# Writing out TensorE's program for 25 tiles with fixed addresses, in place of a loop over a register

## The reference, cut to what matters

```python
h = relu(layernorm(x));  x = x + appnp(h)              # 10 steps: out = spmm(out)*0.9 + h*0.1
h = relu(layernorm(x));  x = x + gat(h, W, att, bias)  # softmax over each node's edges
h = relu(layernorm(x));  x = x + (h + attention(h))    # 4 heads, softmax over each node's edges
h = relu(layernorm(x));  x = x + mean(h[src] @ W + b)  # mean over each node's incoming edges
# spmm: msg = feat[col] * rsqrt(deg_row[row] * deg_col[col]); segment_sum(msg, row)
```

## Time and profile before

| what | value |
|---|---|
| median of 3 runs | 1796.67 us (1793.94 to 1797.15) |
| the profiled execution, its own time | 1796.92 us |
| its span, first to last instruction | 1795.0 us |
| busy share of the span: PE, PEld, DVE, ACT, POOL | 73%, 68%, 71%, 30%, 20% |
| mean granted clock of PE | 0.849 of full |
| counting stage (gathering and counting of all tiles) | about 85 to 373 us of the span |
| the ten steps (L1093) | from 393.6 us to about 922 us |

### The profile page before, as it was taken

One profiled execution on the slowest core, in us unless ns is written; L12 is line 12 of the kernel. 1 busy time (PEld: TensorE's weight loads), 2 busy tenths in 40 slices (PEclk: granted clock), 3 DMA queues, 4 the chain that ended last, 5 costly groups with the idle time before them and its releaser, 6 DMA issues. The chain is left out here.

```text
span 1795.0 us, 46599 instructions
## 1 busy us (share of the span) xinstructions
PE 1313.8 (73%) x18543; PEld 1223.3 (68%) x18544; DVE 1277.8 (71%) x2254; ACT 541.6 (30%) x1073; POOL 361.3 (20%) x202
## 2 busy tenths in 40 slices
PE   3678888849999999999955006777816777777458
PEld 3266777649999999999954005776715777676458
DVE  6876666655555455555565997999877999999832
ACT  0045555520000000000002862333314666666311
POOL 1400000000000000000000004888701555555300
PEclk6867666659999999999986557999858999999779
DMA  0012222258000000000002647555204333333093
GB/s 9 1 51 78 78 78 78 89 197 352 2 3 2 3 2 3 2 2 3 2 1 96 223 140 271 188 203 201 76 3 168 141 130 130 131 130 112 24 343 122
DMA packets 42985, 173.44 MB, mean 97 GB/s; under 512 B 14443, under 2 KB 16020, under 8 KB 42148
## 3 DMA queue, kind: packets, MB, share of 16 engines
q1 hardware_dynamic: 42452, 169.45, 26.0%
q0 software_dynamic: 336, 1.20, 0.2%
HBM read 127.19 MB, written 43.44 MB: 95 GB/s over the span
## 5 line engine op out<-in xcount | busy, mean ns | idle before, releaser
L1093 PE MATMUL psum<-work,count 128*128 128x192 f16 x6250 | 520.6, 247 | 29.6 <-issue 21.5
L1093 PEld LDWEIGHTS psum<-work,count 128*128 128x128 f16 x6250 | 519.0, 98 | 31.4 <-issue 21.7
L1588 PE MATMUL psum<-count 128*128 128x100 f16 (+1 forms) x1875 | 188.3, 208 | 87.8 <-DVE count L1685 61.4
L1038 DVE SCALAR_TENSOR_TENSOR work<-psum,small,work 128x96 f32<-128x96 f32 x250 | 79.4, 318 | 226.5 <-PE psum L1093 226.5
L1588 PEld LDWEIGHTS psum<-count 128*128 128x128 f16 x1875 | 162.6, 98 | 105.4 <-DVE count L1685 56.4
L1360 PE MATMUL psum<-count 128*128 128x98 f16 x625 | 98.4, 210 | 148.6 <-DVE count L1407 109.3
L1653 POOL TENSOR_TENSOR count<-count 128x1000 bf16<-128x1000 f32 (+1 forms) x75 | 166.8, 2224 | 181.9 <-ACT count L1637 181.9
L1399 POOL TENSOR_TENSOR count<-count 128x970 bf16<-128x970 f32 (+1 forms) x75 | 166.7, 2236 | 181.6 <-ACT count L1392 181.6
L1589 PE MATMUL psum<-count 128*128 128x100 f16 (+1 forms) x1875 | 187.2, 207 | 0.0
L878 ACT ACTIVATE work<-work 128x2400 f32<-128x2400 f32 x3 | 6.6, 2202 | 573.8 <-DVE work L865 573.8
L1360 PEld LDWEIGHTS psum<-count 128*128 128x128 f16 x625 | 61.0, 98 | 154.4 <-DVE count L1407 109.5
(11 more groups left out here) (283 smaller groups left out, 2881.4 us busy)
## 6 DMA issues: line engine op xcount, KB each, us to landing
count<-bucket_rows_by_dst SPq DMA_DIRECT2D x50, 800.0 KB, 4.3
count<-bucket_rows_by_src SPq DMA_DIRECT2D x50, 800.0 KB, 4.1
count_f<-count SPq DMA_DIRECT2D x5, 4000.0 KB, 31.0
count<-count_turned SPq DMA_DIRECT2D x25, 800.0 KB, 5.5
count<-count_f SPq DMA_DIRECT2D x17, 800.0 KB, 4.3
count_turned<-x SPq DMA_DIRECT2D x25, 416.0 KB, 2.4
count_turned<-x SPq DMA_DIRECT2D x25, 384.0 KB, 2.4
work<-count_f SPq DMA_DIRECT2D x8, 800.0 KB, 4.2
```

Source lines behind the costliest of these rows:

```text
L1093: last = nc.tensor.matmul(bank[i % BANKS], count16[:, j, i * P:(i + 1) * P], y[par][:, j, :], start=(j == 0), stop=(j == TILES - 1))
L1588: nc.tensor.matmul(slot(b, i, width), hot[:, t0 + i, :], high[:, of, at:at + width], start=True, stop=False, skip_group_check=True)
```

## The change

PE's loop over t = 1 to 23 becomes a loop of Python, so that its 23 passes stand in the program one behind the other, and `block(j)` is given a fixed place in place of one from a register. The waits that were worked out from t are constants too. The inner loop over windows in `place`, the values loaded for each tile, the number and order of matmuls, and the programs of all other engines are left as they were. Line numbers do not move.

```diff
@@ -480,7 +480,7 @@
                 if counts:
                     def block(j):
-                        return count16[:, bass.ds(t - 1, 1), j * P:(j + 1) * P].rearrange("p a n -> p (a n)")
+                        return count16[:, t - 1, j * P:(j + 1) * P]
 
                     if b == 0:
                         for j in range(TILES):
@@ -529,7 +529,7 @@
                     place(n, visit, 1)
                     tile(0, False)
-                    with pe.Fori(1, TILES - 1) as t:
+                    for t in range(1, TILES - 1):
                         lo, n, visit, _ = tile_values(pe, t + 1, True)
                         place(n, visit, t + 1)
                         tile(t)
```

## The result

The changed kernel takes 1734.09 us (median of 4, 1732.54 to 1734.74) where the kernel before took 1795.53 us (median of 4): a ratio of 0.9657, 95% interval 0.9640 to 0.9673, 61 us less. The forecast was 1739.9 us with a range from 1735 us. (The kernel before had a median of 1796.67 us when the forecast was made, 1.1 us more than beside the changed kernel; without this difference the time would lie at the range's end.) The profiled execution took 1732.54 us, with a span of 1730.7 us.

The account below looks back on a forecast made before the run. PE and ACT waiting for each other in the counting stage were taken as the bound, with L487 on that path. 23 x 2.47 = 56.8 us off the 1796.67 us median gave 1739.9 us, other terms nothing; range 1735 to 1753 us.

Parts of the forecast that it names:

- The ring and L487: Counting stage: PE and ACT wait for each other, L487 lies on that path; 2.47 us less a tile, 56.8 us.
- The ring of 8.72 us: Counting stage's period per tile for PE and ACT after the change, in place of 11.19 us.
- rival "more": Transposes (L489) might run at full clock, 0.7 us less a tile; 1738.3 us with DVE holding the stage; chance 0.08.
- The lower bound: L487's gain if only the register operations' own 46 ns are saved: 25 x 46 = 1.15 us a tile.
- The rival built on it: Register operations at L487 cost only what they last: 26.5 us gained, 1770 us; chance 0.04.
- L489 ...: nothing: The 13 transposes take the same in the loop and outside, 1.55 us, so they gain nothing.
- The clock is not what differs: L487's 3.12 us in the loop against 0.67 us outside: both at half clock; 0.63 us at full.
- DVE as the cap: DVE's pass of about 8.6 us in the counting stage would hold it, limiting the full-clock case to 1738.3 us.
- Longer code: About 19 or 20 more instruction packets on q8 while PE runs the written-out passes, costed at nothing.
- I cost them at nothing: The added instruction packets are hidden by arriving ahead; uncovered, 32 us if every one fell on the path.
- a few of those cost 2 us each on DVE, mostly absorbed: SP's ids store, read at DVE's L617: landings of up to 4.3 us occur against the shrunken slack.
- The 0.5 us computed: Slack between the landing of SP's ids store and DVE's L617 after the change, down from 3.0 us.

Follow-up runs that it names:

- e5: Code written out as in the changed kernel, but block(j)'s row comes from a register loaded from the table in each pass; 1801.56 us, 1.0035 of the kernel before.
- e1: Kernel before with its loop kept, but block(j) names one fixed place, row tile 0, in all passes (timing only); 1727.66 us, 0.9621 of the kernel before.
- e8: Changed kernel with each tile's 25 sum matmuls (L487) done twice; 1749.54 us, 0.9743 of the kernel before.
- e10: Kernel before, loop and register addresses kept, with L487's sums moved ahead of PE's wait for ACT's last copy; 1767.28 us, 0.9836 of the kernel before.
- e11: Changed kernel with L487's sums moved ahead of PE's wait for ACT's last copy; 1720.07 us, 0.9580 of the kernel before.
- e6: e3 with 12 idle matmuls in PE's pause ahead of its wait for ACT's last copy; 1725.70 us, 0.9604 of the kernel before.
- e7: e3 with 22 idle matmuls in PE's pause ahead of its wait for ACT's last copy; 1724.00 us, 0.9599 of the kernel before.
- e3: Changed kernel with SP storing the next tile's ids ahead of its wait for ACT's last copy; 1732.44 us, 0.9652 of the kernel before.
- e2: Code written out, row taken from a one-pass loop's register whose value was known when built; 1734.64 us, 0.9659 of the kernel before.

## Why the prediction was right or wrong

*The ring and L487: right.* 56.8 us were forecast for the sums and 57.1 us came, by the two passes outside the loop that showed what the code would cost. The ring of 8.72 us came out too: tiles at half clock are 8.73 to 8.75 us long where the ids aren't late, and those at full clock mostly 7.97 to 8.09 us, the 8.0 us of rival "more". The lower bound, 46 ns an operation, would have given 26.5 us; an operation's own duration is not what it costs the stream behind it (99 ns here). The rival built on it fell with e5 and e1. e8, e10 and e11 show that L487 was on the path for its whole length.

*The step that failed: "L489 ...: nothing".* The 13 transposes were costed at nothing because both rows of them were at half clock. They gained 6.9 us. The text had the mechanism among the rivals, with 0.7 us a tile, but gave it a chance of 0.08, and this is the term that was mis-sized, nothing in place of 6.9 us: it came true in part in 14 of 23 tiles. e6 and e7 show the cause. "The clock is not what differs" was true of L487 (0.67 against 0.63 us) and was silently carried over to L489. The Trainium skill ("TensorE: Matmul & The Clock Gate", Part 1: The HAM clock gate) has the rule that an idle engine falls back to half rate and that activity releases it; the trace agrees: with a pause of 1.2 to 1.7 us left ahead of L487 in most tiles, 14 of 23 have half rate in their transposes, wholly or in part; with the pause filled in e7, all 23 take 0.81 to 0.87 us.

*DVE as the cap: wrong.* Rival "more" was capped at 1738.3 us by a pass of 8.6 us. That pass held 0.79 us of DVE's loads ahead of L617 and 0.33 us ahead of L595. They are DVE's own, as argued, but they are hidden as soon as DVE is late and its sequencer runs ahead: in the pass of the earlier trace rows DVE's load of the tile's values (L409) starts at 284.75 us, behind L644, and in the first pass after the change at 102.95 us, 0.9 us ahead of it. DVE's rows of that pass, and two L644 (L648 there) of e11:

```profile
103.96 0.62 DVE L645 COPY x<-psum 128x896 f16<-128x896 f16 x1
104.50 0.25 DVE L617 TENSOR_SCALAR x<-psum 128x100 f16<-128x100 f32 x1
```
```profile
209.50 0.18 DVE L648 TENSOR_TENSOR x<-x,psum 128x25 f32<-128x25 f32 x1
...
216.64 0.18 DVE L648 TENSOR_TENSOR x<-x,psum 128x25 f32<-128x25 f32 x1
```

The whole pass is 7.14 us when nothing is waited for, against 8.53 us read; the two gaps are 1.12 us of the difference. A gap that an engine has while it waits for others is no part of its shortest pass. This false cap is what kept the range's low end at 1735 us.

*Longer code: right in size, wrong in kind.* 17 more packets came where 19 or 20 were forecast, and PE did not stall for them: the row of the ten steps was the right one to read. But "I cost them at nothing" left out who else uses the DMA engines. They made the landing of the ids late, in tiles where its slack had shrunk from 3.0 us. The 0.5 us computed is right at half clock; at full clock nothing is left, and L617 starts 0.24 to 0.3 us behind a landing even where that took 1.7 us. The prediction had both halves, the slack and the late landings, and joined them only as "a few of those cost 2 us each on DVE, mostly absorbed". And the 4.3 us of the earlier trace rows were read too widely: they are the stage's last store alone, issued at 359.5 us while the load of x (L712, from 352.8 us, landed after 8.6 us) was under way; in the loop no landing was above 1.8 us. The rest of the ring grew by 2.1 us in the trace, and in the versions without packets (e1) or without late landings (e3) it is 4.6 and 2.7 us shorter than in the changed kernel, 1.6 us of e1's spread evenly without a known cause. So the late landings cost 2 to 4 us in all; closer than that it stays open.

*The sum.* 57.1 + 6.9 - 2.1 = 62 us in the stage. The forecast erred by 5 us there: the clock's 6.9 us, less the 2.1 us that the late ids took. Two readings in the working are a little off and change nothing: L617 comes 1.50 us behind L644, not 1.52, and DVE is late by 1.1 us at the start, not 1.2.

## What to carry to other kernels

An address taken from a loop's register can cost more than its register operation lasts: compare with a copy of the same code at fixed places, if the program holds one, and look whether the address alone can be fixed before writing loops out. When a phase between two engines gets shorter, ask which clock the next one will run at; here a pause of 1.2 to 1.7 us ahead of PE's work cost more than idle matmuls in it, as long as these ended before the pause did. And before a second engine is taken for the next bound, take from its pass the gaps that it only has because it waits.

## What the runs showed of the hardware that was not expected

- A register operation of 46 ns ahead of each of 25 one-column matmuls makes the matmul follow at 125 ns in place of 26 ns.
- A packet of PE's instructions (16 KB) that begins in the first 1.2 us of a store of 25 KB goes with a landing after 3.2 to 4.0 us in place of 1.7 us (15 of 15 stores in the changed kernel, e2 and e11); in the loop of the kernel before, without packets, it never was above 1.8 us.
- Idle matmuls, 22 a tile and 1.4 us of work, made 23 tiles 5.8 us shorter than in the same kernel without them (185.71 against 191.55 us).
- DVE's shortest pass (7.14 us) is 1.4 us less than its pass while it waits for PE (8.53 us), because its register loads run ahead only when it is late.
